# Attention output kept as f16 halves, and read back by transposing DMAs as the projection's left operand

## The reference, cut to what matters

```python
x = layernorm(x + self_attention(x))             # 16 heads of 16, 4 groups, per sequence
# cross attention, 8 heads of 128: all 1792 queries against all 6000 keys
q, k, v = heads(x @ Wq), heads(ctx @ Wk), heads(ctx @ Wv)
p = softmax(1.5 * q @ k.T * 128 ** -0.5)
x = layernorm(x + merge(p @ v) @ Wout + bout)
x = layernorm(x + gelu(x @ ternary(W1).T + b1) @ ternary(W2).T + b2)
```

## Time and profile before

| | |
|---|---|
| runs (median; from, to) | 2304.46 us; 2302.53, 2307.41 |
| profiled execution | 2306.85 us, of which the trace spans 2305.1 |
| TensorE busy | 2252.5 us, 98% |
| VectorE busy | 2020.4 us, 88% |
| ScalarE busy | 1865.1 us, 81% |
| GpSimd busy | 1898.6 us, 82% |
| granted TensorE clock | 0.996 of 2.4 GHz |
| DMA moved | 50.44 MB, mean 22 GB/s |

### The profile page before, as it was taken

The page is one execution under the profiler, slowest core; times in us unless marked ns, Lnnn a source line. Parts: engine busy times, 40 slices in busy tenths (PEclk is TensorE's granted clock), DMA queues, the critical chain, the costliest instruction groups (busy, mean ns, idle before and its releaser), DMA issues.

```text
span 2305.1 us, 61948 instructions
## 1 busy us (share of the span) xinstructions
PE 2252.5 (98%) x26078; PEld 1980.7 (86%) x26078; DVE 2020.4 (88%) x2241; ACT 1865.1 (81%) x2224; POOL 1898.6 (82%) x1153
## 2 busy tenths in 40 slices
PE   7998999999999999999999999999999999999998
PEld 4557998899889998899888998899889998998886
DVE  7878988988889888988898898988899888898876
ACT  4357888888888888888878888888888888888855
POOL 8675888888878888888888898888878888899953
PEclk8999999999999999999999999999999999999999
DMA  7400000000000000000000000000000000010220
GB/s 201 158 32 21 6 4 13 4 7 6 11 6 4 7 13 4 6 4 7 13 4 5 6 13 4 6 4 7 13 4 6 4 6 6 4 47 7 90 79 33
DMA packets 34837, 50.44 MB, mean 22 GB/s; under 512 B 2304, under 2 KB 27392, under 8 KB 34560
## 3 DMA queue, kind: packets, MB, share of 16 engines
q1 hardware_dynamic: 34560, 46.46, 6.5%
HBM read 30.99 MB, written 15.47 MB: 20 GB/s over the span
## 4 chain that ended last, share of the span: by engine, by line
PE 71%; POOL 15%; DVE 6%; issue 4%; ACT 3%; POOLq 0%; DVEq 0%; ACTq 0%
PE psum L420 26%; POOL e_lo L1618 12%; PE psum L452 9%; PE psum L445 9%; PE psum L450 5%; PE psum L448 5%; PE psum L567 4%; PE psum L557 4%; POOL e_hi L1612 3%; DVE run_max L1082 3%; ACT ring L847 2%; PE psum L693 2%; PE psum L740 1%; PE psum L529 1%; PE psum L574 1%
## 5 line engine op out<-in xcount | busy, mean ns | idle before, releaser
L1618 POOL TENSOR_TENSOR e_lo<-ring,e_hi 128x1024 f16<-128x1024 f32 (+1 forms) x665 | 1388.8, 2103 | 196.4 <-ACT ring L862 160.8
L1082 DVE TENSOR_TENSOR run_max<-psum,run_max 128x1024 f16<-128x1024 f32 (+1 forms) x616 | 737.9, 1198 | 183.5 <-ACT ring L847 180.3
L847 ACT ACTIVATE ring<-psum 128x1024 f32<-128x1024 f32 (+1 forms) x672 | 673.7, 1003 | 180.0 <-PE psum L420 104.8
L1103 DVE SCALAR_TENSOR_TENSOR ring<-ring,psum 128x1024 f32<-128x1024 f32 (+1 forms) x672 | 792.5, 1186 | 0.7 <-PE psum L660 0.7
L420 PE MATMUL psum<-qx_hi,k_hi 128*128 128x256 f16 x2632 | 718.0, 273 | 15.5 <-DVE run_max L1082 9.1
L420 PE MATMUL psum<-qx_hi,k_lo 128*128 128x256 f16 x2632 | 717.8, 273 | 0.0
L420 PE MATMUL psum<-qx_lo,k_hi 128*128 128x256 f16 x2632 | 717.7, 273 | 0.0
L452 PE MATMUL psum<-v_main,e_lo 128*128 128x129 f16 x4032 | 711.4, 220 | 0.0
L862 ACT ACTIVATE ring<-ring 128x1024 f32<-128x1024 f32 (+1 forms) x672 | 696.1, 1036 | 1.3 <-DVE ring L1103 0.7
L445 PE MATMUL psum<-v_main,e_hi 128*128 128x257 f16 x2016 | 550.4, 273 | 1.3 <-POOL e_lo L1618 1.3
L450 PE MATMUL psum<-v_main,e_hi 128*128 128x128 f16 x2016 | 446.9, 222 | 0.0
(11 more groups left out here) (203 smaller groups left out, 3171.2 us busy)
## 6 DMA issues: line engine op xcount, KB each, us to landing
o_scratch<-o_buf SPq DMA_DIRECT2D x56, 128.0 KB, 1.9
raw<-o_scratch SPq DMA_DIRECT2D x14, 512.0 KB, 4.4
stage<-in_ctxT SPq DMA_DIRECT2D x6, 500.0 KB, 3.9
stage<-in_ctxT SPq DMA_DIRECT2D x12, 250.0 KB, 4.9
w_scratch<-wall SPq DMA_DIRECT2D x1, 2304.0 KB, 10.9
wall<-w_scratch SPq DMA_DIRECT2D x6, 384.0 KB, 3.2
x<-in_xT SPq DMA_DIRECT2D x4, 448.0 KB, 6.6
res<-in_x SPq DMA_DIRECT2D x1, 1792.0 KB, 17.6
```

Source lines behind the costliest of these rows:

```text
L847: a.activation(ring[:, f % SLOTS, 0:n], pair(f)[:, 0:n], ACT.Copy).then_inc(s_kept, 1)
L1082: ins = v.tensor_tensor(run_max[:, 0:n], pair(f)[:, 0:n], run_max[:, 0:n], ALU.max)
L1103: v.scalar_tensor_tensor(slot, slot, LIFT, psum[:, 6, 0:QB].unsqueeze(1).broadcast_to([P, t, QB]), ALU.add, ALU.subtract).then_inc(s_sub, 1)
L1618: g.tensor_tensor(e_lo[f % NEL][:, 0:n], slot, e_hi[f % NEH][:, 0:n], ALU.subtract).then_inc(s_lo, 1)
```

## The change

The output is no longer stored in f32. At the eviction ScalarE writes the first tile in f32 to a small tile `o_first` and the second tile's high half in f16 straight to `o_buf`. VectorE, in `output_halves`, then has four instructions where `add_low` had one: it completes the first tile, makes the second tile's low half from PSUM, casts the first tile to its high half, and subtracts for its low half. SP stores the same 128 KB to a new DRAM tensor of f16 halves.

In the tail a tile is read by `dma_start_transpose`, which lands it with the 128 head columns on the partitions, so that `raw` itself is the projection's left operand. The transposes of raw tiles on TensorE and the two splits per tile on ScalarE and VectorE are gone. There are seven buffers instead of five (two lie where the halves were), freed by the projection; the pairs of tiles use three PSUM banks (6, 0, 1) in turn. The first five projections, not four, lie in the last 15 steps, each three turns earlier; the first two residual additions move from behind the loop to turns 9 and 14, the biases two turns forward, and the other projections move up into the gaps (tile 13 ahead of `down(2)`).

```diff
-        raw = [at(o, f"raw{r}", [P, NH, DH], F32)
-               for r, o in enumerate((VREG, VREG + 4096, WREG, RING, RING + 4096))]
+        raw = [at(o, f"raw{r}", [P, NH, 2, P], F16)
+               for r, o in enumerate((VREG, VREG + 4096, WREG, RING, RING + 4096, KREG + 14336, KREG + 18432))]
...
-        O_TURN = {3 * i: i for i in range(5)}
-        BIASED = {6 + 2 * i: i for i in range(5)}
-        O_PROJECT = {3 * i + 3 + x: (i, range(*w)) for i in range(4) for x, w in enumerate(((0, 3), (3, 6), (6, 8)))}
+        O_PROJECT = {3 * i + x: (i, range(*w)) for i in range(5) for x, w in enumerate(((0, 3), (3, 6), (6, 8)))}
+        BIASED = {4 + 2 * i: i for i in range(5)}
+        RESIDUAL = {9: 0, 14: 1}
...
-            return (7, 3, 2)[p] if p < 3 else 6
+            return (7, 3, 2)[p] if p < 3 else (6, 0, 1)[p % 3]
...
-                def o_transposes(i):
...
                     if heads[0] == 0:
-                        pe.wait_ge(t_lo, i + 1)
+                        pe.wait_ge(s_raw[i % NRAW], 16 * (i // NRAW + 1))
...
-                                           lhsT=o[i % 2][:, h, :], rhs=w[:, h, :],
+                                           lhsT=raw[i % NRAW][:, h, o, :], rhs=w[:, h, :],
...
-                    for t in range(QT):
-                        a.activation(o_buf[:, t, :], psum[:, 4 + n % 2, O_AT[t]:O_AT[t] + DH], ACT.Copy,
+                    for t, dst in enumerate((o_first[:, :], o_buf[:, 1, 0, :])):
+                        a.activation(dst, psum[:, 4 + n % 2, O_AT[t]:O_AT[t] + DH], ACT.Copy,
                                      scale=o_den[:, t:t + 1]).then_inc(s_oev, 1)
...
-                def o_high(i):
...
-                def add_low(n):
-
+                def output_halves(n):
+
+                    bank = psum[:, 4 + n % 2, :]
                     v.wait_ge(s_oev, n * QT + QT)
-                    v.scalar_tensor_tensor(o_buf[:, 0, :], psum[:, 4 + n % 2, OW:VW], o_den[:, 0:1], o_buf[:, 0, :],
-                                           ALU.mult, ALU.add).then_inc(s_olo, 1)
+                    v.scalar_tensor_tensor(o_first[:, :], bank[:, OW:VW], o_den[:, 0:1], o_first[:, :],
+                                           ALU.mult, ALU.add).then_inc(s_whole, 1)
+                    v.scalar_tensor_tensor(o_buf[:, 1, 1, :], bank[:, O_AT[1]:O_AT[1] + DH], o_den[:, 1:2],
+                                           o_buf[:, 1, 0, :], ALU.mult, ALU.subtract).then_inc(s_whole, 1)
+                    v.wait_ge(s_whole, 2 * n + 1)
+                    v.tensor_copy(o_buf[:, 0, 0, :], o_first[:, :]).then_inc(s_ohi, 1)
+                    v.wait_ge(s_ohi, n + 1)
+                    v.wait_ge(s_whole, 2 * n + 2)
+                    v.tensor_tensor(o_buf[:, 0, 1, :], o_first[:, :], o_buf[:, 0, 0, :],
+                                    ALU.subtract).then_inc(s_olo, 1)
...
-                def o_low(i):
...
                     if i >= NRAW:
-                        sp.wait_ge(t_tr, i - NRAW + 1)
-                    sp.dma_start(raw[i % NRAW][:, :, :].rearrange("p h d -> p (h d)"),
-                                 o_part[i * P:(i + 1) * P, :]).then_inc(s_raw[i % NRAW], 16)
+                        sp.wait_ge(t_wp, i - NRAW + 1)
+                    sp.dma_start_transpose(raw[i % NRAW][:, :, :, :].rearrange("p h x t -> p (h x) t"),
+                                           halves_dram[i * P:(i + 1) * P, :]).then_inc(s_raw[i % NRAW], 16)
```

More of the change, by code:

```diff
@@ L103, in build @@
         SMALL = FOLD + 512
-        assert SMALL + 1216 <= SBUF
+        assert SMALL + 1568 <= SBUF
         yT_hi = at(0, "yT_hi", [P, 2, NT], F16)
@@ L128, in build @@
         t_dram = nc.dram_tensor("t_scratch", (4, P, W12), F16, kind="Internal").ap()
+        halves_dram = nc.dram_tensor("halves_scratch", (NT, NH * 2 * DH), F16, kind="Internal").ap()
         res = at(RING + 12 * 4096, "res", [T, NB, D], F32)
         res2 = at(KREG, "res2", [P, NT // P, D], F32)
-        o_part = o_dram[:, 0:INNER]
         res_dram = o_dram[:, INNER:INNER + D]
@@ L250, in build @@
         row_max = at(SMALL, "row_max", [P, QT], F16)
-        o_den = at(SMALL + 32, "o_den", [P, QT], F32)
-        o_buf = at(SMALL + 160, "o_buf", [P, QT, DH], F32)
+        o_den = at(15616, "o_den", [P, QT], F32)
+        o_buf = at(SMALL + 32, "o_buf", [P, QT, 2, DH], F16)
+        o_first = at(SMALL + 1056, "o_first", [P, DH], F32)
         LATE, LOW_AHEAD = NF_ALL - 14, 2
         s_lo_odd = sem("b_lo_odd")
-        (s_qk, s_kept, s_max, s_sub, s_hi, s_exp, s_cast, s_lo, s_av, s_fold2, s_fold, s_bc, s_den, s_oev, s_olo, s_od,
-         s_init) = [
+        (s_qk, s_kept, s_max, s_sub, s_hi, s_exp, s_cast, s_lo, s_av, s_fold2, s_fold, s_bc, s_den, s_oev, s_whole,
+         s_ohi, s_olo, s_od, s_init) = [
             sem("b_" + n) for n in ("qk", "kept", "max", "sub", "hi", "exp", "cast", "lo", "av", "fold2", "fold",
-                                    "bc", "den", "oev", "olo", "od", "init")]
+                                    "bc", "den", "oev", "whole", "ohi", "olo", "od", "init")]
         s_side, s_half, s_free = sem("b_side"), sem("b_half"), sem("b_free")
@@ L346, in build @@
         w2t = w12t[:, W12:2 * W12].rearrange("p (k n) -> p k n", k=NF)
-        oT_hi = [at(KREG + 14336 + 2048 * r, f"oT_hi{r}", [P, NH, P], F16) for r in range(2)]
-        oT_lo = [at(KREG + 18432 + 2048 * r, f"oT_lo{r}", [P, NH, P], F16) for r in range(2)]
         norm2 = [at(o, f"norm2_{r}", [P, D], F32) for r, o in enumerate((QREG, QREG + 1024, RUN, RUN + 1024))]
@@ L389, in columns @@
             return (FIRST[c + 1] - FIRST[c]) * P
-        (t_bias, t_tr, t_hi, t_lo, t_wp, t_n, t_cp, t_n3, t_add, t_nt, t_yh, t_yl, t_f1, t_ge, t_hh, t_hl, t_f2, t_add2,
+        (t_bias, t_wp, t_n, t_cp, t_n3, t_add, t_nt, t_yh, t_yl, t_f1, t_ge, t_hh, t_hl, t_f2, t_add2,
          t_bn, t_bn2, t_ag, t_sq, t_ag3, t_sq3, t_shift,
          t_n3a, t_last, t_out) = [
-            sem("t_" + n) for n in ("bias", "tr", "hi", "lo", "wp", "n", "cp", "n3", "add", "nt", "yh", "yl", "f1", "ge",
+            sem("t_" + n) for n in ("bias", "wp", "n", "cp", "n3", "add", "nt", "yh", "yl", "f1", "ge",
                                     "hh", "hl", "f2", "add2", "bn", "bn2", "ag", "sq", "ag3", "sq3", "shift", "n3a", "last",
@@ L684, in o_project @@
                             pe.wait_ge(s_late, 48)
+                        elif i == 2:
+                            pe.wait_ge(s_max, NF_ALL)
                         elif i == 6:
                             pe.wait_ge(s_sub, NF_ALL)
-                        elif i % 2 == 0 and p >= 4:
-                            pe.wait_ge(t_add, p)
+                        elif i == 12:
+                            pe.wait_ge(t_add, 4)
                     for h in heads:
-                        for n, (o, w) in enumerate(((oT_hi, wout_hi), (oT_hi, wout_lo), (oT_lo, wout_hi))):
+                        for n, (o, w) in enumerate(((0, wout_hi), (0, wout_lo), (1, wout_hi))):
                             mm = pe.matmul(psum[:, bank_of_projection(p), (i % 2) * D:(i % 2 + 1) * D],
-                                           lhsT=o[i % 2][:, h, :], rhs=w[:, h, :],
+                                           lhsT=raw[i % NRAW][:, h, o, :], rhs=w[:, h, :],
                                            start=(h == 0 and n == 0), stop=(h == NH - 1 and n == 2))
@@ L796, in _ @@
                 blocks((NH - 2) * NQB, NBLK)
-                o_transposes(5)
-                o_project(4)
-                o_transposes(6)
+                o_project(5)
                 n_transposes(0)
-                o_project(5)
-                o_transposes(7)
+                o_project(6)
                 n_transposes(1)
-                o_project(6)
+                o_project(7)
                 for c in range(2):
@@ L808, in _ @@
                     up(c, range(0, 4))
-                    o_transposes(i)
-                    o_project(i - 1)
+                    o_project(i)
                     up(c, range(4, 8))
-                    o_transposes(i + 1)
-                    o_project(i)
+                    o_project(i + 1)
                     down(2 * c)
+                    n_transposes(2 * c + 2)
                     if c == 0:
[L816 to L819, removed]
+                        o_project(i + 2)
                         down(1)
                         n_transposes(3)
-                        o_transposes(i + 3)
-                        o_project(i + 2)
+                        o_project(i + 3)
                     else:
@@ L1399, in last_norms, with first_residual @@
                                         ALU.subtract, ALU.mult).then_inc(t_last, 1)
+                def first_residual(p):
+                    of = res2[:, 2 * p:2 * p + 2, :]
+                    v.wait_ge(t_bias, 2 * p + 2)
+                    v.wait_ge(t_wp, 2 * p + 2)
+                    v.scalar_tensor_tensor(of, psum[:, bank_of_projection(p), :].rearrange("p (i d) -> p i d", i=2),
```

(4 more changed lines are left out.)

43 lines of the change are left out of this document (7 added, 36 removed).

## The result

The changed kernel takes 2396.48 us (median of 4 runs, 2395.49 to 2396.63), the kernel before 2305.93 beside it on the same chip (4 runs, 2302.53 to 2307.49): ratio 1.0387, interval 1.0374 to 1.0399. The forecast was 2372, with 2318 to 2460 as its range.

The account below looks back on a forecast made before the run. TensorE was taken as the bound, with VectorE's spare time only in small pieces. Profiled 2306.85 + 74.6 for the loop - 9.4 for the tail, transposing DMAs 0, gave 2372 us; range 2318 to 2460.

Parts of the forecast that it names:

- The collision: At the eviction: VectorE's new subtraction stands still until GpSimd's instruction ends; next instruction 2.8 us late per block.
- The loop's term: Attention loop: the part of the evictions' delay that reaches TensorE, 74.6 us in sum, bounds 0 and 154.
- the forecast's 2.4: Last head: GpSimd waits for the new instructions, then for late exponentials; 2.4 us per block, six blocks.
- one block of the first kind: Attention loop, blocks that do not make the next keys: one walked, 1.4 us each reaches TensorE, 34 blocks.
- The tail's gain: Tail: TensorE loses raw-tile transposes, 12.2 us, less stalls of 1.2 and 1.6: gain 9.4 us.
- The stall before the first norm's transposes: Tail, behind the last attention step: TensorE's projections cover too little of the first norms' 4.5 us chain; 1.2 us.
- The third chunk's up projection: Tail: with projection 13 moved ahead, VectorE's chain to this projection ends 1.6 us behind TensorE.
- Rival D: Last steps: GpSimd's pace keeps the tail's gain to 5 us, 2377 us; counted within the forecast's 0.62.
- The transposing DMAs: Tail loads: taken to land like plain loads, at a cost of 0, with 0 and 50 us as ends.
- Rival C: Tail: slow transposing loads add 50 us at 10 us a tile, 2422 us; chance 0.12.
- A: Attention loop: VectorE's spare time swallows the whole delay, 2297 us, faster; chance 0.11.
- B: Attention loop: the whole delay reaches TensorE because every fold collides, 2451 us; chance 0.12.

Follow-up runs that it names:

- the eviction alone: Kernel before plus only VectorE's three extra instructions per block, into a scratch tile nothing reads; f32 store and tail untouched: 2405.51 us, ratio 1.0431.
- the first variant: Changed kernel with the first tile's completed value written back to its PSUM bank, where cast and subtraction read it: 2298.82 us, ratio 0.9965.

## Why the prediction was right, and which term was too small

**The collision** happened as forecast: subtraction 2.25 us, 2.79 us late per block (forecast 2.8), and only in the form and place that the theory names. The Trainium skill's rule of a full block ("SBUF — State Buffer", section "Who interferes with whom") is borne out by the runs with the operand in PSUM (291 ns) and with the subtraction moved (1744 ns); the statement of the Trainium skill there that a tensor_reduce never contends on this chip agrees with the fold's reduction, 1925 to 2004 ns.

**The loop's term was too small:** 74.6 us against 96.6 with the eviction alone. Against the kernel before, by the query block in which the eviction's delay is spent (blocks of a head counted from 0, means over the heads that make values and keys), the eviction-only run is longer by:

| query block | 0 | 1 | 2 | 3 | 4 | 5 | 6 |
|---|---|---|---|---|---|---|---|
| us per block | 3.1 | 1.4 | 1.3 | 1.3 | 2.8 | 0.8 | 0.7 |
| forecast | 1.4 | 1.4 | 1.4 | 1.4 | 1.4 | 0.9 | 0.9 |

In the last head the forecast's 2.4 stands beside 2.3 to 2.5, with 3.3 in its first block and 5.1 and 1.9 in its last two. The forecast walked one block of the first kind and took it for all five. It fits three, and in its steps too: with the eviction alone the scores of blocks 2 and 3 come about 0.25 us late (forecast 0.35), the transposes 0.4 (0.6) and the spreading 1.2 to 1.3 (1.5). Of the 22.0 us that are missing, block 0 (six times) and block 4 (seven times) make 10.2 and 9.6, the last head makes 5.4, and the other blocks lie 3.2 under the forecast. Part of the last head's 5.4 is a slip in the sum: 34 + 14 + 6 are 54 blocks, where the loop has 55.

In block 0 both halves of the fold collide. The kernel after, VectorE, GpSimd and TensorE in order of time there:

```profile
488.04 2.29 DVE L1054 TENSOR_TENSOR run_max<-run_max 128x512 f16<-128x512 f16 x1
490.36 2.10 DVE L1057 TENSOR_TENSOR fold<-run_max 128x256 f16<-128x256 f16 x1
...
487.90 4.40 POOL L1578 TENSOR_TENSOR e_lo<-ring,e_hi 128x1024 f16<-128x1024 f32 x2
...
492.51 0.28 PE L655 MATMUL psum<-ident,fold 128*128 128x128 f16 x2 [1.93 <-DVE fold L1057]
```

The same two instructions of the same block in the kernel before:

```profile
476.94 0.41 DVE L1087 TENSOR_TENSOR run_max<-run_max 128x512 f16<-128x512 f16 x1
477.39 1.01 DVE L1090 TENSOR_TENSOR fold<-run_max 128x256 f16<-128x256 f16 x1
```

Each now waits for one of GpSimd's pair, and TensorE waits 1.93 us for the second. Where the fold is one reduction, block 0 loses only 0.7; and in the fifth head's block 0, where the first half happens to stay at 0.41, the kernel after loses 0.8 instead of 3.2 to 3.9 (this block took 0.7 longer than its like already before). In the second, third and fourth head TensorE's granted clock falls behind this wait, from 2.4 to 1.2 GHz; in the sixth and seventh it does not. One such stretch, with the columns of the earlier trace rows:

```profile
494.00:497.00 3.00, 2.53 (x16) 1.71 (x14) 3.00 (x5) 0.20 (x1) 2.47 (x2) 0.50 0.00 0
```

The three heads in which it falls lose 0.7 to 0.9 us more in blocks 0 and 1 together than the two that keep the clock: about 2.5 us in all, for which the forecast had no term. That is a comparison of blocks; no run tested it.

In block 4 the first half of the fold went from 0.45 to 1.00 and the second from 1.01 to 2.11, but there the reduction leaves 1.6, so the fold is not all of it. The rest is the scores. Values are made in blocks 0 to 3, and block 4's first side product, a key product, comes in step 9; so TensorE reaches the second scores behind the eviction 3.6 us after it, where it takes 5.2 in blocks 1 to 3. In the kernel after they wait 1.8 to 1.9 us for the running maximum in block 4 of each of the seven heads; one of them, its eviction at 624.37:

```profile
629.93 0.28 PE L424 MATMUL psum<-qx_hi,k_hi 128*128 128x256 f16 x1 [1.89 <-DVE run_max L1049]
```

With the eviction alone these scores come 2.0 us late, and with the reduction 2.0 as well. So block 4 is of another kind than blocks 1 to 3, and it is the first of three, not two, that make keys. Blocks 5 and 6 lose least: their fold's second half had taken 2.1 us before.

In four of the last head's blocks the size was right, but the forecast's path to it, through GpSimd and late exponentials, is not shown: from one eviction to the next (2108.0 to 2144.1 of the kernel after) TensorE's own waits for VectorE at scores, transposes and spreading, 1.2, 0.5 and 0.7 us, already come to 2.4.

**The tail's gain was right in sum:** 9.4 forecast; the changed kernel's span is 2393.7 against 2403.3 with the eviction alone, 9.6 us, and the first variant's median lies 8.6 us under the kernel before. In its parts it was less exact. Two rows of the kernel after, from its waits in the tail:

```profile
PE psum L703 <- DVE norm L1301: 2.8, 1, 2.8
...
PE psum L715 <- DVE yT_lo L1307: 1.2, 1, 1.2
```

The stall before the first norm's transposes was 2.8 us for 1.2, and 2.4 with the collision gone, so the chain was under-counted by about one microsecond beside the 0.4 that the collision adds. The third chunk's up projection waits 1.2 for 1.6. Rival D, that GpSimd's pace holds the gain to 5 us, fell.

**The transposing DMAs cost nothing,** as taken. The kernel after, issue on SP's queue (ns) and issue to landing:

```profile
L1638 SPq DMA_TRANSPOSE raw<-halves_scratch x14: 1428/2470/3365, 2255.3 to 2316.1; - x14
...
DMA to landing us min/median/max: 4.6/5.1/6.4
```

A tile of sixteen 128x128 blocks lands in 5.1 us, inside the plain loads' 3.4 to 7.1 of the earlier trace rows (their median is 4.4), and no row of the waits has TensorE waiting for a tile or GpSimd for the residual. Rival C fell. The rule of the Trainium skill in "Advanced Engine Details and Errata", section "X-Bar Transpose (TRN2)", that such transfers are as fast as plain ones agrees with this to within the 0.7 us between the medians. The forecast's estimate of 21 us a tile, sixteen times the 1309 ns that the Trainium skill has for one block in "VectorE: DVE Perf Modes", section "The three transpose paths", does not: the measured 5.1 us decide against adding the blocks up.

**Rivals A and B.** A (all swallowed) holds at 0.8 us of delay and not at 1.7 or 2.8. B's condition, that every fold collides, came about in nearly every block (the second half's median is 2.1 us); its price was too high, because about one of the 2.8 us does not reach the end: 96.6/55 is 1.8 per block.

## What to carry to other kernels

Before a short instruction is put on VectorE, look at where its operands lie and what GpSimd runs at that moment: with both inputs in SBUF its price here was the rest of GpSimd's instruction, and a delay in one piece larger than the bound engine's margin pushed later instructions of the same kind into the next collision. Keeping one operand in PSUM made the same work free here. When one block is walked to price a loop, walk one of each kind whose side work differs: block 4, without side work in its first steps, lost twice what the walked block did.

## What the runs showed that was not expected

The price has a threshold: 0.6 to 0.8 us of delay per block cost nothing, 1.7 us cost 41, 2.8 us cost 97. Two instructions that are free alone are dear together: in the rows above the first one's wait carries the second past the gap ahead of GpSimd's low half, some 0.08 us wide (588.90 to 588.98). Last, a transposing load holds SP's queue at its issue. The first three of the kernel after, in order of time, took 7.08 us where the three plain ones of the earlier trace rows had taken 1.37; nothing waited for them here.

```profile
2255.35 7.08 SPq L1638 DMA_TRANSPOSE raw<-halves_scratch  x3
```
